# Moving five residual additions from VectorE to GpSimd in a two-layer graph kernel

## What is computed

```python
def reference(x, adj, W, a):                      # x 4096 x 128, adj 4096 x 4096 of 0 and 1
    h = maximum(layernorm(x), 0)
    x = x + max over the neighbours j of h[j]     # layer 0, the "neighbour maximum"
    h = maximum(layernorm(x), 0)
    x = x + elu(softmax(mask(leaky(h W a1 + (h W a2)^T))) h W)   # layer 1, graph attention
    return x
```

## Time and profile before

| what | value |
|---|---|
| median of the runs | 795.0 us |
| profiled execution, its time | 794.1 us |
| its span, first to last instruction | 792.1 us |
| TensorE busy | 706.9 us (89%) |
| VectorE busy | 723.0 us (91%) |
| ScalarE busy | 486.0 us (61%) |
| GpSimd busy | 283.7 us (36%) |
| mean granted TensorE clock | 0.988 |

### The profile page before, as it was taken

The page is one execution under the profiler, slowest core; times in us unless marked ns, Lnnn a source line. Parts: engine busy times, 40 slices in busy tenths (PEclk is TensorE's granted clock), DMA queues, the critical chain, the costliest instruction groups (busy, mean ns, idle before and its releaser), DMA issues.

```text
span 792.1 us, 14762 instructions
## 1 busy us (share of the span) xinstructions
PE 706.9 (89%) x5592; PEld 483.2 (61%) x5592; DVE 723.0 (91%) x1120; ACT 486.0 (61%) x615; POOL 283.7 (36%) x258
## 2 busy tenths in 40 slices
PE   1688999999999999999999999779889999999995
PEld 1344544444444444444444444469789999999995
DVE  8899889999999999999999999999968899998894
ACT  2978888888888888888888888364241221010000
POOL 0612033443443443443443444453320075232030
PEclk9999999999999999999999999899999999999998
DMA  9799777897777777777777763724433434444410
GB/s 305 240 373 364 263 249 221 271 327 222 240 257 215 247 239 228 250 248 215 255 233 227 258 206 91 262 69 149 130 112 120 146 135 170 153 157 160 149 40 16
DMA packets 62856, 162.55 MB, mean 205 GB/s; under 512 B 6400, under 2 KB 11136, under 8 KB 58688
## 3 DMA queue, kind: packets, MB, share of 16 engines
q1 hardware_dynamic: 53776, 138.75, 50.6%
q0 software_dynamic: 9008, 22.82, 11.8%
HBM read 117.51 MB, written 44.04 MB: 204 GB/s over the span
## 4 chain that ended last, share of the span: by engine, by line
PE 46%; ACT 21%; DVE 20%; issue 8%; DMA 2%; POOL 1%; ACTq 0%; DVEq 0%; SPq 0%
PE pick_ps L678 22%; PE pick_ps L578 9%; ACT edge_t L373 9%; DVE acc L836 8%; PE order_ps L559 6%; ACT depth L382 6%; DVE rest L1015 5%; ACT first L381 4%; PE late_ps L591 3%; PE late_ps L550 2%; DVE rest L825 2%; DMA subset_max<-keys 1%; PE late_ps L587 1%; PE late_ps L657 1%; DVE acc L944 1%
## 5 line engine op out<-in xcount | busy, mean ns | idle before, releaser
L836 DVE TENSOR_TENSOR acc<-pick_ps,acc 128x1024 f32<-128x1024 f32 x248 | 302.9, 1222 | 27.6 <-PE pick_ps L578 21.3
L345 POOL DMA_INDIRECT found<-subset_max,entry x192 | 206.3, 1074 | 296.0 <-DVE entry L848 195.7
L1015 DVE SCALAR_TENSOR_TENSOR rest<-depth,curves_sb,stage 128x512 f32<-128x512 f32 x256 | 200.9, 821 | 21.6 <-PE pick_ps L678 5.5
L678 PE MATMUL pick_ps<-keys,rest 128*128 128x129 f32 x1792 | 208.0, 277 | 4.5 <-DVE rest L1015 3.5
L678 PEld LDWEIGHTS pick_ps<-keys,rest 128*128 128x128 f32 x1792 | 204.6, 193 | 9.2 <-DVE rest L1015 6.3
L381 ACT ACTIVATE first<-order_ps,neg 128x1024 f16<-128x1024 f32 x128 | 142.7, 1115 | 60.7 <-PE order_ps L559 57.7
L382 ACT ACTIVATE depth<-order_ps,mid 128x1024 f16<-128x1024 f32 x128 | 141.7, 1107 | 0.0
L373 ACT ACTIVATE edge_t<-late_ps 128x1024 f16<-128x1024 uint16 x128 | 131.1, 1024 | 2.9 <-PE late_ps L550 2.9
L559 PE MATMUL order_ps<-edge_t,order_w 128*128 128x512 f16 x256 | 79.2, 392 | 39.3 <-ACT edge_t L373 31.9
L578 PE MATMUL pick_ps<-first,h_hi 128*128 128x512 f16 x256 | 98.4, 384 | 6.0 <-DVE acc L836 5.9
L550 PEld LDWEIGHTS late_ps<-ident_h,stage 128*128 128x128 f16 x1024 | 69.3, 100 | 49.1 <-DMA stage<-adj 13.3
(11 more groups left out here) (140 smaller groups left out, 575.3 us busy)
## 6 DMA issues: line engine op xcount, KB each, us to landing
stage<-adj SPq DMA_DIRECT2D x64, 1024.0 KB
edge_units<-edge_t SPq DMA_DIRECT2D x64, 512.0 KB
stage<-edge_units SPq DMA_DIRECT2D x32, 1024.0 KB, 4.9
subset_max<-keys POOLq DMA_DIRECT2D x12, 512.0 KB, 8.6
found<-subset_max,entry POOLq DMA_INDIRECT x192
best<-x SPq DMA_DIRECT2D x4, 512.0 KB, 6.3
subset_max<-x POOLq DMA_DIRECT2D x4, 512.0 KB, 8.6
out<-keys POOLq DMA_DIRECT2D x7, 256.0 KB, 3.3
```

What stands on the lines that cost most here:

```text
L345: nc.gpsimd.indirect_dma_start(found[:, n % NG, s, :], None, subset_max, bass.IndirectOffsetOnAxis(entry[:, n, s:s + 1], 0)).then_inc(gath ...
L678: last = nc.tensor.matmul(out_ps(q, b), weight[:, n % WEIGHTS, b * P:(b + 1) * P], wh[:, c, :], start=c == 0 and starts(q, b), stop=c == C ...
L836: V.tensor_tensor(acc[:, q % 2, :], pick_ps[k][:, :], acc[:, q % 2, :], ALU.max).then_inc(raised, 1)
L1015: V.scalar_tensor_tensor(out=weight[:, n % WEIGHTS, :], in0=limit[:, q % 4, :], scalar=slope[:, c:c + 1], in1=units[:, m % EDGES, k * TI:( ...
```

## The change

The additions of tiles 2 to 6 leave VectorE's program. GpSimd gets an `add` of its own, in two instructions instead of one: first `left` is multiplied by 1/HSCALE in place, then, behind a wait for the new semaphore `left_scaled`, it is added to `x1`. Tiles 2 and 3 are added in front of the fetches of block 28, tiles 4, 5 and 6 in front of those of block 30. Tiles 0, 1 and 7 stay on VectorE.

```diff
@@ gpsimd
+                def add(g):
+                    pool.wait_ge(joined, g + 1)
+                    xg = x1[:, g * ROWS:(g + 1) * ROWS, :].rearrange("p c d -> p (c d)")
+                    lg = left[:, g * ROWS:(g + 1) * ROWS, :].rearrange("p c d -> p (c d)")
+                    nc.gpsimd.tensor_scalar(lg, lg, 1.0 / HSCALE, None, ALU.mult).then_inc(left_scaled, 1)
+                    pool.wait_ge(left_scaled, g - 1)
+                    nc.gpsimd.tensor_tensor(xg, xg, lg, ALU.add).then_inc(x1_made, 1)
+
                 for n in range(C):
+                    if n == LAST * ROWS:
+                        add(2)
+                        add(3)
+                    if n == LAST * ROWS + 2:
+                        add(4)
+                        add(5)
+                        add(6)
@@ vector
-                    if n in (2, 3):
-                        add(n)
@@
                     if n in (24, 27):
                         merge(n // 3 - 4)
-                        add(n // 3 - 4)
@@
                     if n == 31:
                         merge(6)
-                        add(6)
```

More of the change, by code:

```diff
@@ L220, in layers @@
         small_put, small_took = sem("small_put"), sem("small_took")
+        left_scaled = sem("left_scaled")
         mom_made, std_made, scaled, step = sem("mom_made"), sem("std_made"), sem("ln2_scaled"), sem("ln2_step")
```

## The result

The changed kernel takes 798.79 us in the median of 12 runs (796.88 to 800.53), the kernel before 795.16 (791.67 to 796.68, 12 runs). The ratio, estimated over all runs, is 1.0058, with a 95% interval of 1.0045 to 1.0070: slower by 3.6 to 5.6 us. It is not the quotient of the two medians, which is 1.0046 (+3.6 us). The profiled execution took 799.05 us, its span 797.0 instead of 792.1 (+4.9).

The account below looks back on a forecast made before the run. The prediction took VectorE's program to set the pace up to step 40 (571.78). From 794.1 us profiled, + 1.4 + 1.0 + 1.4 gave 797.9 us, or 798.8 by the median, with a range of 794.2 to 801.2.

Parts of the forecast that it names:

- The stage: Up to step 40 (571.78) VectorE sets the pace; a microsecond lost or gained there is paid or earned in full.
- Tiles 2 and 3: Statistics of tile 3 wait for GpSimd's addition and start at 528.6 instead of 527.21: +1.4 us.
- Tiles 4 and 5: Tile 4 does not wait; statistics of tile 5 start at 559.3 instead of 556.91: +1.0 us, together +2.4.
- the mark of 552.2: GpSimd's late arrival at tile 4's addition costs nothing as long as it is before 552.2 us.
- the second rival: Fetches of blocks 28 and 29 keep the whole shift, ending at 555.3, so additions run late: 800.8 us, chance 0.14.
- Tile 6: Statistics of tile 6 wait for an addition of 3.20 us, starting at 565.6 instead of 561.80: +1.4, together +3.8.
- The disturbance: Each moved addition slows VectorE's weight tiles by up to 1.4 us; not added where VectorE would wait anyway.
- the rival with short additions: GpSimd's tensor_scalar takes 0.69 us, an addition 2.4: +2.0, 796.1 us, chance 0.08.
- Behind: After tile 6 the shift stays; block 31's fetches end at about 587, covered by some 15 us before first use.
- The clock: TensorE idles about 3.1 us at `stat(6)` and its clock falls again: some +1.1, 799.0 us, chance 0.20.
- the likeliest case: VectorE's waits for GpSimd before statistics of tiles 3, 5 and 6 give 797.9 us, just within 0.5%; chance 0.53.

Follow-up runs that it names:

- The first run above: Only the additions of tiles 2 and 3 on GpSimd, those of 4 to 6 back on VectorE; ratio 1.0012 to the kernel before.
- The run with late statistics: The changed kernel, all five additions on GpSimd, with the statistics of tiles 3 to 6 later in VectorE's loop; ratio 1.0012 to the kernel before.
- the load alone: The kernel before, additions on VectorE, with GpSimd doing the same five instruction pairs on a buffer nobody reads; ratio 1.0047 to the kernel before.
- tile 4 early: The changed kernel with the addition of tile 4 moved in front of the last two fetches of block 29; ratio 1.0051 to the kernel before.
- the run with tiles 4 to 6 alone: Only the additions of tiles 4 to 6 on GpSimd, those of 2 and 3 back on VectorE; ratio 1.0027 to the kernel before.

## Why the prediction held, point by point
- **The stage.** The time follows from when VectorE comes to step 40, and a shift there is paid in full: +3.9 on VectorE and +4.7 on TensorE at step 40, +4.9 at the end.
- **Tiles 2 and 3.** Forecast +1.4, measured 528.40 less 527.21, +1.2. The first run above shows that this term is not fixed: with the fetch 1.5 us sooner it was about 0.1.
- **Tiles 4 and 5.** Forecast +1.0, measured +1.3 (559.40 less 556.91 is 2.5 in all). Two errors met here. The additions were shorter than the 3.43 us taken, 2.84 us: their tensor_tensors, 1.27 us, ran beside a waiting VectorE, and their tensor_scalars took 1.49. And GpSimd was later, 553.5 for the end of block 29 and not 551.9, behind the mark of 552.2. The forecast let block 29 start right behind block 28; its first fetch stood 1.85 us for a landing, which before had been hidden in the 3.17 us of wait for VectorE. So the second rival, GpSimd late, happened in a mild form: 1.5 us of waiting for tile 4 that the forecast did not have. That the errors nearly cancelled, +0.3 in the term, was luck.
- **Tile 6.** Forecast +1.4 with an addition of 3.20; measured +1.4 (3.91 in all) with one of 3.3.
- **The disturbance.** Forecast at up to 1.4 us per addition and not added to the waits. The trace has 1.7 in all, 1.4 of it before the wait for tile 3, where the forecast had counted either the one or the other. The run with late statistics shows that it takes the waits' place when they go, but only in part: the prediction says that the steps in front cannot fill a wait, and there they filled 5.65 us of waits at a price of 2.1. With the load alone it was 0.7 us per addition, half of the 1.4.
- **Two readings.** The pair of weight tiles of 1.77 us ran within a second tensor_scalar of GpSimd (646.95 to 648.88), not only beside the end of one. And 0.69 us is VectorE's scalar_tensor_tensor; a tensor_scalar of this shape took it 0.50 at 521.25, so the rival with short additions priced GpSimd's too high even by its own rule. Neither enters the sum.
- **Behind.** The last fetch of block 31 ended at 589.1 (587 forecast) and its rows were first used at 606.10, without a wait, as said.
- **The clock.** Given 0.20 as a rival, at +1.1. It happened: a gap of 3.26 us (3.1 forecast), a fall, 0.7 us in the profile. This is the step of the likeliest case that failed: it was made with a full clock, though the gap that its own waits would make was near in length to the one of 3.70 us behind which the profile already showed a fall. With it the sum is 797.9 + 0.7 = 798.6, against 799.05 for the profiled execution.
- **The size.** +3.8 forecast; measured +3.6 between the medians, +4.6 by the ratio, +4.9 between the profiled executions. By the ratio it lies beyond the 0.5% that the likeliest case was put just within, by the medians not. That the prediction's 798.8, its figure by the median, is the measured median to 0.01 us is luck: its sum leaves out the clock, and the two errors above met in it.

Open is why the clock falls behind one gap and not behind its like. The profile with late statistics has the gap of 3.70 us at 585.39 and no fall behind it; that with tile 4 early has falls behind gaps of 2.78 and of 1.88 us, where one of 1.76 in the changed kernel has none. The fall that the changed kernel shows from 521 to 528 is in some runs and not in others, and cost VectorE's chain nothing. So single profiles of this kernel may differ by 1.5 us for that alone.

## What to carry to other kernels
An engine that takes over an elementwise instruction has to be fast enough for the next reader, and its own earlier work counts too: ask when the result is wanted, not only whether the engine is idle. In this kernel GpSimd's additions were not beside VectorE's work but in its way, so moving 3.3 us of VectorE to GpSimd cost 3.8 or more in the versions with all five moved, as waiting or as slowed instructions. The gaps of 3.3 and 3.7 us on TensorE were paid twice in all traces but one, once as idle time and once as a lower clock, unless they were filled; filling the one of 3.7 with matmuls that nobody needs was worth 1.7 us here.

## What was not expected of the hardware
- A VectorE instruction's delay beside a GpSimd tensor_tensor can be many times its own length: a 128x6 copy of 0.17 us took 2.39 us behind two tensor_tensors of GpSimd, and about 2.4 in a second run. A search (MAX8 over 1024 columns) that ran beside a tensor_tensor of GpSimd in the run with tiles 4 to 6 alone was not slowed: 1.21 us, as before.
- GpSimd's tensor_tensor of an addition took 1.26 or 1.27 us beside a VectorE that waited, and up to 1.71 otherwise. Its tensor_scalar took 1.49 to 1.97 us, and the short ones were not those beside an idle VectorE: at 553.61 and 556.53 VectorE was working.
- At gaps of TensorE of 3.26 and 3.27 us the lower clock lasted 3.4 us in one profile, from behind the gap, and 6.8 us in another, from within it.
